# The last addition of a fused block is made by TensorE in PSUM instead of by VectorE

## The chip, the cores and the metric

The kernel runs on one core of one Trainium2 chip. A core has a matrix engine (TensorE, PE in the profile; its weight loads are PEld), three engines for element work (VectorE or DVE, ScalarE or ACT, GpSimd or POOL) and an engine that issues most DMAs (SyncE or SP). All have their own instruction lists and wait for one another by semaphores. The metric is the device time of one execution in microseconds; less is better.

## The reference, cut to what matters

`x` has 16 batches of 256 rows of 128 numbers. The block is an attention of the delta-rule kind with gates, and then a layer in which each row goes to one of eight experts:

```python
x = x + ga * attn(layernorm(x) * (1 + ca) + sa)
h = layernorm(x) * (1 + cb) + sb
route = softmax(h @ router_w + router_b)
y = (silu(h @ w1[e][:, :512]) * (h @ w1[e][:, 512:])) @ w2[e]     # e: the row's best expert
x = x + gb * (y * max(route))
```

`ga` and `gb` are gates, one vector of 128 numbers for each batch. The change concerns the last line, for half of the rows.

## The kernel before, in words

The 256 rows of a batch are cut into two slices of 128 rows, s = 0 and s = 1. A slice holds 16 tiles of 128 rows (one for each batch). The attention runs as a scan over time in which all engines take part; it fills the first two thirds of the span. Behind it comes the expert layer. The rows of a slice are sorted by expert into 23 padded tiles of 128 rows (NF = 23, so G = 46 tiles in all), with scatters to DRAM (`sorted_h`). For each tile g SyncE loads the rows, TensorE turns them (`turn_x`, L888), multiplies by the expert's first matrix (`hidden`, L900), ScalarE and VectorE make the gated product, TensorE multiplies by the second matrix (`second`, L917), VectorE copies the result out of PSUM (L2012), and GpSimd scatters the tile's rows back to their places in DRAM (`placed_y`, L1143).

When all tiles of a slice are back in DRAM, its 16 tiles are loaded again in four quarters q = 0 to 3 of four tiles, 256 KB each (`load_y`, L326), into YG. VectorE then finishes each quarter (`finish`): for slice 1 a product with the gates GB, which already hold the routing weight (L2027), and a sum with the residual rows XG (L2030). SyncE stores the quarter (`store_out`, L330). For slice 0 this happens while the tiles of slice 1 run. For slice 1 it is the end of the program: nothing else is left to do.

Each engine's list is written out by hand, and its order in the program is the order in which that engine works. The order between engines comes from semaphores alone: `y_in` (a quarter has landed), `dve_link` (VectorE's product is written and its own sum may read it), `out_ready` (a quarter is ready), `att_ps` and `x1_ready` (used earlier for the attention's results, four times for slice 1). At the end TensorE's list has nothing behind the last tile's `second`, and ScalarE's nothing behind the last `silu` (L1494).

Another line matters for prices: `project` (L636) multiplies 128x128 weights by 512 columns, three times for each of NB = 8 blocks; it is the form that the new matmuls have. `copy_x1` (L1360) is ScalarE's copy of one PSUM bank of 512 columns into four tiles of X, made for slice 0.

PSUM has eight banks of 128 x 512 numbers, bank[0] to bank[7]. The expert layer uses banks 0 and 4 for turned rows, 1, 2, 6 and 7 for the first product, 3 and 5 for results.

Of the kernel before, what the change touches and what calls it, by code (L numbers as in the profile page):

```python
# [8 lines left out]
ALU = mybir.AluOpType  # L9
ACT = mybir.ActivationFunctionType  # L10
# [8 lines left out]
def adaln_block(nc, x, Wq, Wk, Wv, Wo, Wbet, Wf, norm_w, router_w, router_b, w1, w2, c, wmod, out):  # L19
# [81 lines left out]
    with ExitStack() as ctx:  # L101
        def sb(name, shape, dt=F32):
            return ctx.enter_context(nc.sbuf_tensor(name, shape, dt))
# [3 lines left out]
        def sem(name, h=None):  # L107
            key = name if h is None else f"{name}{h}"
            if key not in sems:
                sems[key] = ctx.enter_context(nc.semaphore(key))  # L110
            return sems[key]
# [27 lines left out]
        ID = sb("ID", [P, P])  # L139
# [45 lines left out]
        bank = [ctx.enter_context(nc.psum_tensor(f"bank{i}", [P, 512], F32)) for i in range(8)]  # L185
# [4 lines left out]
        BACK_BANKS = [[bank[4]] * 4, TURN_BANKS[1]]  # L190
        LG_BANK = [bank[5][:, 0:NT * E], bank[0][:, P:P + NT * E]]
        RANK_BANK = [bank[4], bank[4]]


        def turned(g):
            return bank[4 if g >= TWO_X and g % 2 else 0][:, 0:P]
# [4 lines left out]
        def place_before(g, two):  # L201
            return g - 2 if g > two else g - 1
# [5 lines left out]
        def staged_k(h, n):  # L208
# [18 lines left out]
        YG = [[K_[h][:, s * P:(s + 1) * P, :].rearrange("p t d -> p (t d)").rearrange("p (n d) -> p n d", n=HB)  # L227
               for h in range(NHALF)] for s in range(NTIME)]
# [4 lines left out]
        XG = [X[:, :, :].rearrange("p (b s) d -> p s b d", s=NTIME)[:, s, :, :] for s in range(NTIME)]  # L233
# [18 lines left out]
        GB = WOG  # L252
# [73 lines left out]
            queue.dma_start(YG[s][q // 2][:, q % 2 * 4:q % 2 * 4 + 4, :], rows).then_inc(sem(f"y_in{q}"), 16)  # L326

        def store_out(queue, s, q):
            queue.wait_ge(sem("out_ready"), 4 * s + q + 1)
            queue.dma_start(out_t[s][:, 4 * q:4 * q + 4, :], XG[s][:, 4 * q:4 * q + 4, :]).then_inc(sem("stored"), 16)  # L330

        def shifted(queue, k):
# [140 lines left out]
        def _(sp):  # L473
# [116 lines left out]
            for q in range(4):  # L590
                store_out(sp, 1, q)
# [4 lines left out]
        def _(pe):  # L596
# [143 lines left out]
            def attend(s, q):  # L740

                h = q // 2
                if q % 2 == 0:
                    pe.wait_ge(sem(f"ot_in{h}_", s), 16 * (SHARE if (s, h) == (1, 0) else HB))
                if s == 1 and q == 0:
                    pe.wait_ge(sem("ot_pool0_", 1), 16 * (HB - SHARE))
                if s == 1 and q == 0:
                    pe.wait_ge(sem("pos_ready"), 1)
                    pe.wait_ge(sem("oh_ready"), 1)
                if s == 1 and q >= 2:  # L750
                    pe.wait_ge(sem("x1_ready", 1), q - 1)
                for i in range(4):
                    b = 4 * q + i
                    ps = ATT_BANKS[s][q][:, i * P:(i + 1) * P]
                    m = pe.matmul(ps, OT[h][:, b % HB, :], WOG[:, b, :], start=True, stop=(s == 1))
                    if s == 0:
                        m = pe.matmul(ps, ID[:, :], XG[0][:, b, :], start=False, stop=True)
                m.then_inc(sem("att_ps", s), 1)

            def turn_rows2(k):  # L760

                s, q = divmod(k, 4)
                if s == 0 and q >= 2:
                    pe.wait_ge(sem("router_in"), 4 * (q - 1))
                elif s == 0 or q < 2:
                    pe.wait_ge(sem("xn2_ready", s), 4 * (q + 1))
                if k == 0:
                    pe.wait_ge(sem("x1_ready", 0), 4)
                if s == 0 and q >= 2:
                    shifted(pe, k - 2)  # L770
                elif s == 1 and q >= 2:
                    pe.wait_ge(sem("act_rows"), NT // 2 + q - 1)
                for i in range(4):
                    m = pe.transpose(TURN_BANKS[s][q][:, i * P:(i + 1) * P], XNB[:, 4 * q + i, :], ID[:, :])
                m.then_inc(sem("xn2t_ps"), 1)
# [30 lines left out]
            def rank(s):  # L806
# [4 lines left out]
                else:  # L811
                    pe.wait_ge(sem("act_rows"), NT // 2 + 3)
                ohf = oh[:, :, :].rearrange("p t e -> p (t e)")
                pe.matmul(RANK_BANK[s][:, 0:NT * E], LOWER[:, :], ohf, start=True, stop=True)
                pe.matmul(RANK_BANK[s][:, NT * E:2 * NT * E].rearrange("p (e t) -> p e t", e=E), ONES[:, :],
                          oh[:, :, :].rearrange("p t e -> p e t"), start=True, stop=True).then_inc(sem("rank_ps"), 1)
# [65 lines left out]
            def turn_x(g):  # L882
                pe.wait_ge(sem(f"xs_in{g % XR}"), 16 * (g // XR + 1))
                if g == TWO_X:
                    pe.wait_ge(sem("pos_ready"), NTIME)
                elif g >= 1:
                    pe.wait_ge(sem("xst_ready"), place_before(g, TWO_X) + 1)
                pe.transpose(turned(g), XS[:, g % XR, 0:D], ID[:, :]).then_inc(sem("xt_ps"), 1)  # L888
# [17 lines left out]
            def second(g):  # L906
                s, j = divmod(g, NF)
                if j == 0:
                    pe.wait_ge(sem("tex_ready"), s + 1)
                expert = pe.value_load(tex[s][0:1, j:j + 1], min_val=0, max_val=E - 1)  # L910
                pe.wait_ge(sem("gu_ready"), g + 1)
                if g == TWO_Y:
                    pe.wait_ge(sem("act_rows"), NT // 2 + 4)
                elif g >= 1:
                    pe.wait_ge(sem("ys_ready"), place_before(g, TWO_Y) + 1)
                for c in range(FC):
                    m = pe.matmul(result(g), GU[g % 3][:, c * P:(c + 1) * P], W2[:, bass.ds(expert, 1), c, :],  # L917
                                  start=(c == 0), stop=(c == FC - 1))
                m.then_inc(sem("y_ps"), 1)

            for g in range(2):
                turn_x(g)
            for g in range(G + 2):
                if g == NF:
                    second(g - 2)
                    for k in range(2):
                        turn_x(g + k)
                if g < G:
                    hidden(g)
                if g == F_ATTEND[1] + 1:  # L930
                    for q in (2, 3):
                        attend(1, q)
                if g == F_TURN + 1:
                    for q in (0, 1):
                        turn_rows2(4 + q)
                if g == F_TURN + 2:
                    for q in (0, 1):
                        weigh_experts(4 + q)
                        turn_rows2(6 + q)
                if g == F_TURN + 3:  # L940
                    for q in (2, 3):
                        weigh_experts(4 + q)
                if g == F_ROUTE + 1:
                    rank(1)
                    turn_x(g + 2)
                if g >= 2 and g != NF:
                    second(g - 2)
                if g == F_ATTEND[0]:
                    for q in (0, 1):
                        attend(1, q)  # L950


        @block.gpsimd
# [204 lines left out]
        def _(act):  # L1158
# [367 lines left out]
            for g in range(G):  # L1526
# [17 lines left out]
                if g == NF - 1:  # L1544
                    exponentials(1)


        @block.vector
        def _(dve):
# [310 lines left out]
            def totals(s):  # L1860

                ranks, at = RANK_BANK[s], 3 * NT * E
                return ranks[:, NT * E:2 * NT * E], ranks[:, at:at + E]

            def sort(s):

                ranks = RANK_BANK[s]
                first = ranks[:, 2 * NT * E:2 * NT * E + E]
# [16 lines left out]
            def sorted_places(s):  # L1885

                ranks = RANK_BANK[s]
                first = ranks[:, 2 * NT * E:2 * NT * E + E]
# [125 lines left out]
            def finish(s, q):  # L2014

                if s == 0 and q == 0:
                    dve.wait_ge(sem("gb_in"), 16)
                dve.wait_ge(sem(f"y_in{q}"), 16 * (s + 1))
                yg = YG[s][q // 2]
                if s == 0:  # L2020
                    for b in range(4 * q, 4 * q + 4):
                        last = dve.scalar_tensor_tensor(out=yg[:, b % HB, :], in0=yg[:, b % HB, :], scalar=maxp[s][:, b:b + 1],
                                                        in1=GB[:, b, :], op0=ALU.mult, op1=ALU.mult)
                else:

                    y4 = yg[:, q % 2 * 4:q % 2 * 4 + 4, :]
                    last = dve.tensor_tensor(y4, y4, GB[:, 4 * q:4 * q + 4, :], ALU.mult)  # L2027
                link(last)
                xr = XG[s][:, 4 * q:4 * q + 4, :]
                dve.tensor_tensor(xr, xr, yg[:, q % 2 * 4:q % 2 * 4 + 4, :], ALU.add).then_inc(sem("out_ready"), 1)  # L2030
# [5 lines left out]
            for g in range(G + 3):  # L2036
# [14 lines left out]
                if g - 1 in F_ATTEND:  # L2051
                    q = 2 * F_ATTEND.index(g - 1)
# [4 lines left out]
                if g - 2 in F_ATTEND:  # L2057
                    q = 2 * F_ATTEND.index(g - 2) + 1
# [58 lines left out]
```

## Time and profile before

| what | us |
|---|---|
| runs shown | 468.97, 472.88, 473.53 (median 472.88) |
| the profiled execution | 471.62 |
| its span | 469.9 |
| last matmul of the last tile ends | 455.1 |
| first quarter of slice 1 has landed | 461.72 |
| last sum on VectorE ends | 467.14 |

The profile is one execution of its own; its span runs from the first to the last instruction, and the execution's time has 1.7 us more around it. In rows of the profile "L2030" is line 2030 of the program, `out<-in` are tiles by the program's names, and an idle time stands with what ended it.

### The profile page before, as it was taken

To read this page: it belongs to the slowest core of one execution; us is meant where nothing else is said; L and a number is where in the kernel's file an instruction comes from. 1 tells how busy PE (TensorE), PEld (TensorE's weight loads), DVE (VectorE), ACT (ScalarE), POOL (GpSimd) and SP (SyncE) were. 2 spreads that over 40 slices of the span, in tenths; PEclk is the share of its full clock that TensorE was granted. 3 is DMA by queue.
4 is the path that set the end of the run, shared out by engine and by line. 5 is a ranking of instruction groups with operands and counts; after the bars stand their busy time and mean duration, and the time that the engine had idled before them with its cause. 6 is when DMAs were issued, how large, how long until landed. Compare 5 with 4: busy or idle time off the path is not lost.

```text
span 469.9 us, 8624 instructions
## 1 busy us (share of the span) xinstructions
PE 371.7 (79%) x2495; PEld 321.4 (68%) x2495; DVE 377.1 (80%) x1143; ACT 281.8 (60%) x634; POOL 276.1 (59%) x339
## 2 busy tenths in 40 slices
PE   3867861947979996892968957879799999999970
PEld 2322320746766776892967857879699998999970
DVE  4868999999999999999998899785718444469634
ACT  3698876857357565577655545374855557556520
POOL 1037235999999949839496288512284546563340
PEclk9979886788879998997896786999989999999995
DMA  8185979990000004905000004127311114155006
GB/s 230 37 117 102 115 111 131 127 114 1 0 1 1 1 1 160 353 27 116 21 0 2 0 13 129 48 63 169 117 30 38 42 37 112 44 163 143 31 34 179
DMA packets 49502, 37.13 MB, mean 79 GB/s; under 512 B 11088, under 2 KB 45200, under 8 KB 49328
## 3 DMA queue, kind: packets, MB, share of 16 engines
q1 hardware_dynamic: 46064, 30.39, 32.9%
q0 software_dynamic: 3392, 6.18, 4.2%
q8 instruction: 21, 0.34, 0.3%
q14 instruction: 25, 0.20, 0.2%
HBM read 17.36 MB, written 10.29 MB: 59 GB/s over the span
## 4 chain that ended last, share of the span: by engine, by line
DVE 33%; PE 29%; POOL 16%; issue 10%; ACT 5%; DMA 5%; SPq 1%; ACTq 0%; POOLq 0%; DVEq 0%
PE bank L900 10%; DVE U L1794 5%; DVE S L1807 5%; PE bank L917 5%; DVE p L1788 4%; DVE p L1801 4%; PE bank L693 3%; PE bank L636 3%; POOL sorted_h L1085 3%; POOL big L1019 3%; DMA sorted_h<-X,pos 2%; DVE big L1724 2%; DVE X L1726 2%; POOL X L987 2%; POOL placed_y L1143 1%
## 5 line engine op out<-in xcount | busy, mean ns | idle before, releaser
L693 PE MATMUL bank<-prod_o,ID 128*128 128x128 f32 x512 | 75.2, 308 | 28.9 <-POOL prod_o L315 17.0
L900 PE MATMUL bank<-Q,p 128*128 128x128 f32 x736 | 95.0, 277 | 0.0
L693 PEld LDWEIGHTS bank<-prod_o,ID 128*128 128x128 f32 x512 | 70.3, 219 | 31.7 <-POOL prod_o L315 20.3
L900 PEld LDWEIGHTS bank<-Q,p 128*128 128x128 f32 x736 | 89.9, 194 | 0.2
L1312 ACT ACTIVATE p<-S,GAM 128x64 f32<-128x64 f32 x126 | 48.6, 412 | 65.6 <-DVE S L1807 64.8
L308 POOL TENSOR_TENSOR prod_o<-Q,ST 128x1024 f32<-128x1024 f32 x28 | 60.0, 2142 | 29.9 <-PE bank L697 29.7
L1143 POOL DMA_INDIRECT placed_y<-Q,place x46 | 44.3, 964 | 51.4 <-DVE place L2000 15.3
L1507 ACT ACTIVATE p<-big 128x1024 f32 x46 | 48.5, 1057 | 42.0 <-PE bank L900 39.4
L1807 DVE TENSOR_REDUCE S<-p 128x64 f32<-128x320 f32 x126 | 55.4, 470 | 0.0
L1794 DVE TENSOR_REDUCE U<-p 128x32 f32<-128x288 f32 x128 | 51.8, 436 | 0.0
L1788 DVE TENSOR_TENSOR p<-S,bank 128x256 f32<-128x256 f32 x128 | 48.3, 405 | 0.7 <-ACT bank L1307 0.7
L1801 DVE TENSOR_TENSOR p<-U,bank 128x256 f32<-128x256 f32 x126 | 47.1, 405 | 0.0
L1085 POOL DMA_INDIRECT sorted_h<-X,pos x32 | 30.9, 965 | 20.5 <-issue 7.8
L636 PE MATMUL bank<-ph,WP 128*128 128x512 f32 x48 | 30.0, 775 | 13.5 <-ACT ph L1197 13.5
L2005 DVE TENSOR_TENSOR S<-S,bank 128x512 f32<-128x512 f32 x31 | 21.2, 685 | 18.7 <-PE bank L900 14.2
L917 PE MATMUL bank<-big,S 128*128 x248 | 33.6, 281 | 2.8 <-ACT Q L1514 2.8
L697 PEld LDWEIGHTS bank<-prod_o,ID 128*128 128x128 f32 x256 | 35.2, 213 | 0.0
L697 PE MATMUL bank<-prod_o,ID 128*128 128x128 f32 (+3 forms) x256 | 34.8, 284 | 0.0
L315 POOL TENSOR_TENSOR prod_o<-PD,U 128x128 f32<-128x128 f32 (+1 forms) x112 | 33.8, 341 | 0.0
L1998 DVE COPY Q<-bank 128x128 f32<-128x128 f32 x46 | 13.2, 287 | 25.6 <-PE bank L888 25.4
L917 PEld LDWEIGHTS bank<-big,S 128*128 128x128 f32 x248 | 30.7, 196 | 3.3 <-issue 3.3
L636 PEld LDWEIGHTS bank<-ph,WP 128*128 128x128 f32 x48 | 10.7, 241 | 27.7 <-ACT ph L1197 15.5
(265 smaller groups left out, 755.0 us busy)
## 6 DMA issues: line engine op xcount, KB each, us to landing
big<-in_L_ffn_w_dram SPq DMA_DIRECT2D x1, 4096.0 KB, 14.2
big<-big SPq DMA_DIRECT2D x16, 192.0 KB, 5.0
Q<-sorted_h SPq DMA_DIRECT2D x46, 64.5 KB, 2.0
sorted_h<-ZERO SPq DMA_DIRECT2D x2, 1472.0 KB, 18.5
X<-in_L_attn_x_dram SPq DMA_DIRECT2D x8, 256.0 KB, 4.5
big<-big SPq DMA_DIRECT2D x16, 128.0 KB, 5.3
K<-placed_y SPq DMA_DIRECT2D x8, 256.0 KB, 4.3
out_dram<-X SPq DMA_DIRECT2D x8, 256.0 KB, 2.4
```

Source lines behind the costliest of these rows:

```text
L308: engine.tensor_tensor(slot[:, 0:HD, :, :, :], q, states.unsqueeze(3).broadcast_to(full), ALU.mult)
L636: m = pe.matmul(bank[1 + i][:, :], WP[:, i, :], rhs, start=True, stop=True)
L693: pe.matmul(ps, ID[:, :], prod_o[:, k % 2, i, :], start=(i == 0), stop=False, skip_group_check=True)
L697: m = pe.matmul(o4, ID[:, :], r4, start=False, stop=(d == C - 1), skip_group_check=True)
L900: m = pe.matmul(bank[(1, 6)[g % 2] + k][:, c * P:(c + 1) * P], W1E[g % 2][:, f:f + P], XST[:, g % 3, :], start=True, stop=True)
L917: m = pe.matmul(result(g), GU[g % 3][:, c * P:(c + 1) * P], W2[:, bass.ds(expert, 1), c, :], start=(c == 0), stop=(c == FC - 1))
L1143: pool.indirect_dma_start(placed_y[g // NF], bass.IndirectOffsetOnAxis(ap=place[:, g:g + 1], axis=0), YS[:, g % YR, :], None).then_inc(sem ...
L1312: act.activation(p2[h][:, :, :, C], S_[h][:, n % SR, :, :], ACT.Copy, scale=GAM[h][:, n:n + 1])\
L1788: dve.tensor_tensor(p1[h][:, n % UR, :, :, 0:HD], s_, w, ALU.mult).then_inc(sem("seq_w", h), 1)
L1794: dve.tensor_reduce(U_[h][:, n % VR, :, :], p1[h][:, n % UR, :, :, :], AX_X, ALU.add)\
L1801: dve.tensor_tensor(p2[h][:, :, :, 0:C], u, k, ALU.mult).then_inc(sem("state_in", h), 1)
L1807: dve.tensor_reduce(S_[h][:, (n + 1) % SR, :, :], p2[h][:, :, :, :], AX_X, ALU.add).then_inc(sem("s_ready", h), 1)
```

## The change

For slice 1 alone. TensorE gets eight more matmuls behind its last tile. Four (`residuals`) multiply the identity by the residual rows of a quarter, 512 columns, into banks 0, 4, 1 and 2, and open an accumulation there; they wait for nothing. Four (`add_results`) each wait until VectorE has multiplied the quarter by the gates, and multiply the identity by that product into the same bank, so that it is added to the residual rows. VectorE's sum of slice 1 is gone, and so is its wait for its own product; `out_ready` now comes from the product. ScalarE copies each finished bank into X behind its last `silu`, and the stores of slice 1 wait for these copies. Loads, stores and slice 0 stay as they are.

```diff
+        OUT_BANKS = [bank[i][:, :] for i in (0, 4, 1, 2)]
...
         def store_out(queue, s, q):
-            queue.wait_ge(sem("out_ready"), 4 * s + q + 1)
+            if s == 0:
+                queue.wait_ge(sem("out_ready"), q + 1)
+            else:
+                queue.wait_ge(sem("x1_ready", 1), 4 + q + 1)
...
+            def residuals(q):
+                pe.matmul(OUT_BANKS[q], ID[:, :], XG[1][:, 4 * q:4 * q + 4, :], start=True, stop=False)
+
+            def add_results(q):
+                pe.wait_ge(sem("out_ready"), 4 + q + 1)
+                pe.matmul(OUT_BANKS[q], ID[:, :], YG[1][q // 2][:, q % 2 * 4:q % 2 * 4 + 4, :], start=False, stop=True)\
+                    .then_inc(sem("att_ps", 1), 1)
...
+            for q in range(4):
+                residuals(q)
+            for q in range(4):
+                add_results(q)
...
+            for q in range(4):
+                act.wait_ge(sem("att_ps", 1), 4 + q + 1)
+                act.activation(XG[1][:, 4 * q:4 * q + 4, :], OUT_BANKS[q].rearrange("p (n d) -> p n d", n=4), ACT.Copy)\
+                    .then_inc(sem("x1_ready", 1), 1)
...
                     y4 = yg[:, q % 2 * 4:q % 2 * 4 + 4, :]
-                    last = dve.tensor_tensor(y4, y4, GB[:, 4 * q:4 * q + 4, :], ALU.mult)
+                    dve.tensor_tensor(y4, y4, GB[:, 4 * q:4 * q + 4, :], ALU.mult).then_inc(sem("out_ready"), 1)
+                    return
```

VectorE's list at the end of the program before, with what each instruction waits for (K is the tile that holds YG, X holds the residual rows):

```order
L2027 TENSOR_TENSOR K<-K,ph 128x512 [waits y_in0]
L2030 TENSOR_TENSOR X<-X,K 128x4x128 [waits dve_link]
L2027 TENSOR_TENSOR K<-K,ph 128x512 [waits y_in1]
L2030 TENSOR_TENSOR X<-X,K 128x4x128 [waits dve_link]
L2027 TENSOR_TENSOR K<-K,ph 128x512 [waits y_in2]
L2030 TENSOR_TENSOR X<-X,K 128x4x128 [waits dve_link]
L2027 TENSOR_TENSOR K<-K,ph 128x512 [waits y_in3]
L2030 TENSOR_TENSOR X<-X,K 128x4x128 [waits dve_link]
```

And the same place now (the program's lines have moved down by 22 there):

```order
L2049 TENSOR_TENSOR K<-K,ph 128x512 [waits y_in0]
L2049 TENSOR_TENSOR K<-K,ph 128x512 [waits y_in1]
L2049 TENSOR_TENSOR K<-K,ph 128x512 [waits y_in2]
L2049 TENSOR_TENSOR K<-K,ph 128x512 [waits y_in3]
```

The sums are gone and the products stand directly behind one another. TensorE's list at its end now, behind the last tile (L921 is `second`; before, the list ended with it):

```order
L921 ISA
L921 MATMUL bank<-big,S 128x128
L921 ISA
L921 MATMUL bank<-big,S 128x128
L928 MATMUL bank<-X,ID 128x512 x4
L932 MATMUL bank<-K,ID 128x512 [waits out_ready] x4
```

The four matmuls of L928 carry no wait and follow the tile at once; those of L932 wait for VectorE's products one by one.

## Rows read from the trace of the kernel before

**Rows 1.** The page: the span, and TensorE's granted clock in 40 slices.
```profile
span 469.9 us, 8624 instructions
...
PEclk9979886788879998997896786999989999999995
```

**Rows 2.** The chain of waits, 459 to 470 us: start, us, what.
```profile
461.74 0.70 DVE K L2027
...
462.47 0.69 DVE X L2030
...
463.80 0.69 DVE X L2030
...
465.12 0.69 DVE X L2030
...
466.45 0.69 DVE X L2030
```

**Rows 3.** Timeline of SyncE's queue, 466.9 to 469 us: start, us, line, operation.
```profile
467.17 0.37 SPq L330 DMA_DIRECT2D out_dram<-X  x1
```

**Rows 4.** Line L330, the stores: from issue to landing.
```profile
DMA to landing us min/median/max: 2.3/2.4/2.4
```

**Rows 5.** Line L326, the loads, 455 to 470 us: issue (ns, first and last start), landing.
```profile
L326 SPq DMA_DIRECT2D K<-placed_y x4: 370/504/507, 458.8 to 460.3; - x4
...
DMA to landing us min/median/max: 3.4/4.2/4.4
```

**Rows 6.** Timeline of TensorE, 455 to 470 us: all that it holds.
```profile
454.83 0.28 PE L917 MATMUL bank<-big,S 128*128 x1
```

**Rows 7.** Stretches of TensorE: length, busy time (instructions), granted clock, DMA share, GB/s.
```profile
26.20:30.50 4.30, 0.00 (x0) 0.91 1.12 137
30.60:36.50 5.90, 5.90 (x7) 0.50 0.67 70
...
45.40:46.70 1.30, 1.30 (x3) 1.00 1.14 132
46.80:50.10 3.30, 3.30 (x5) 0.50 1.15 131
65.90:67.90 2.00, 0.00 (x0) 1.00 0.35 40
...
281.40:285.70 4.30, 4.30 (x20) 0.50 0.32 100
337.50:340.20 2.70, 0.00 (x0) 1.00 0.10 24
340.40:343.70 3.30, 3.30 (x16) 0.50 0.06 20
...
459.90:469.80 9.90, 0.00 (x0) 0.50 0.73 210
```

**Rows 8.** Line L636, whole run, then 29 to 37 us: ns min/median/max.
```profile
L636 PE MATMUL bank<-ph,WP x48: 592/594/1219, 15.7 to 70.2; 128*128 128x512 f32 x48
...
L636 PE MATMUL bank<-ph,WP x6: 1057/1057/1219, 30.5 to 35.0; 128*128 128x512 f32 x6
```

**Rows 9.** Timeline: six passes of L636 at full clock, two weight loads at half.
```profile
53.05 2.74 PE L636 MATMUL bank<-ph,WP 128*128 128x512 f32 x6
...
31.55 0.33 PEld L636 LDWEIGHTS bank<-ph,WP 128*128 128x128 f32 x1 [0.52 <-issue]
32.40 0.33 PEld L636 LDWEIGHTS bank<-ph,WP 128*128 128x128 f32 x1 [0.52 <-issue]
```

**Rows 10.** The chain of waits, 308.5 to 309.8 us: VectorE to TensorE and back.
```profile
308.98 0.14 issue
309.11 0.32 PE bank L888
309.43 0.02 issue
```

**Rows 11.** Line L1360, ScalarE's copy of a bank to X.
```profile
L1360 ACT ACTIVATE X<-bank x4: 587/597/629, 225.4 to 232.0; 128x512 f32<-128x512 f32 x4
```

## The prediction

> **What bounds the kernel now.** The page comes first [rows 1]: the span is 469.9 us, no engine fills it, and no engine's share says what the last microseconds cost. They are read from the chain of waits [rows 2]. After TensorE and VectorE have finished the last tile, GpSimd's last scatter lands in DRAM; SyncE then issues four loads, and the first one's landing, at 461.72, starts VectorE. From there the chain is VectorE alone: a product, 0.02 us, a sum, and the next product overlapping the sum's end, four times, a period of 1.33 us (462.47, 463.80, 465.12, 466.45 are the sums' starts). The last sum ends at 466.45 + 0.69 = 467.14. SyncE issues the last store at 467.17 [rows 3] and it lands 2.3 us later [rows 4], at 469.47; 0.4 us of closing semaphores end the span. So what the change can move is the 5.42 us from 461.72 to 467.14, with 2.7 us of landing and closing behind it.
>
> Two other rows limit what can be won there. The loads are issued at 458.8 to 460.3 and land in 3.4 to 4.4 us [rows 5]: the fourth at about 460.3 + 4.4 = 464.7. So no chain can multiply the last quarter before 464.7; today VectorE reaches it at 465.73 (the last sum's start less 0.72), about 1 us after it came. And TensorE, which the change brings in, does its last pass from 454.83 to 455.11 [rows 6] and is idle from there to the end, at half clock from 459.9 on [rows 7].
>
> **What is removed.** Four sums on VectorE of 0.69 us each, and four waits of a sum for its product. VectorE's four products then start as fast as it takes them or as the loads land: the first is ready at 462.44, and the last at about 464.7 + 0.69 = 465.4, against the last sum's 467.14 now. That is the most there is to win, 1.75 us, and what comes behind the product has to fit in it.
>
> **What is added, first half: the residual rows.** Four matmuls of 128x512 with the identity, which wait for nothing and are queued directly behind TensorE's last tile. Their price is the projection's, L636, the only 128x512 form in the trace. Its source line stands at 24 matmuls in the program (three for each of eight blocks) and 48 records in the trace [rows 8]: an fp32 matmul runs in two passes. At full clock six passes take 2.74 us [rows 9] with a last one of 0.59, so (2.74 - 0.59) / 5 = 0.43 us per pass and 0.86 per matmul. Four matmuls are 8 passes, 3.4 us, from 455.1 to about 458.6. I cost them at nothing: VectorE's first product isn't there before 462.44, and nobody else waits on TensorE. Were all of it at half clock (6.8 us) it would end at 461.9 and still be covered.
>
> **What is added, second half: the results.** Four more such matmuls, each waiting for its product; these are on the path. Behind the first one stand the other three, ScalarE's copies wait for them in turn, and SyncE's stores for the copies. The hand-over from VectorE to a waiting TensorE was 0.14 us with its weight load, and back 0.02 [rows 10]. So the first starts at 462.44 + 0.14 = 462.58. What the eight passes take depends on the clock. At half clock the weight loads of the passes, which follow the passes one for one, start 0.85 us apart (31.55, 32.40) [rows 9], and a pass takes 1.06 when its end is counted in, the first of a stretch 1.22 [rows 8].
>
> The clock at 462.58 is the question. TensorE will have idled 4.0 us, from 458.6. In the trace there are 13 stretches of 2.4 us and more without a matmul between 26 us and 341 us, of which [rows 7] shows the first and the last; half clock came in each of them or at most 1.4 us after work resumed (45.4 to 46.7 was that longest delay, still at full clock). The idle stretch of 2.0 us at 65.9 left the clock alone. A stretch of 4.0 belongs to the first kind. Once down, the clock stayed there under full work for 3.3 us (340.4 to 343.7), 4.3 us (281.4 to 285.7) and 5.9 us (30.6 to 36.5) before it rose. So:
> - Longest: half clock through all eight passes. 462.58 + 0.16 (first pass) + 7 x 0.85 + 1.06 = 469.75.
> - Shortest: 1.4 us at full clock (3.3 passes), 3.3 us at half (3.9), the last 0.8 at full (0.35 us): 5.05 us, and 0.16 for the end of the last pass: 467.8.
> - Middle: half for 4.3 to 5 us (5.0 to 5.9 passes), the rest at full (1.3 to 0.9 us): about 5.8 us with 0.3 for the two ends: 468.7.
>
> In all three TensorE is later than the products (the last is ready at 465.4), so it, not VectorE or the loads, sets the end of this part. The Trainium skill, "TensorE: Matmul & The Clock Gate", section "Why this matters for your kernels", speaks against this placement: it counts idle gaps between bursts of matmuls as a way to lose the clock, and shows a loop whose matmuls all run cold behind a wait for a DMA. The trace agrees, by its thirteen stretches.
>
> **What is added, third: the copies out.** ScalarE's copy of one bank to rows of X is the form of L1360, 0.60 us [rows 11]; ScalarE is idle then. Three of the four lie beside TensorE's next matmul, the last is on the path. With 0.02 us before and after, the last store is issued 0.64 us after TensorE's end: at 470.4 (longest), 468.45 (shortest), 469.35 (middle), against 467.17 now. Its landing is costed as today, 2.3 us: the stores come 0.86 us or more apart, against 1.33 today, which showed no queueing; I allow the last 0.1 us behind the one before, inside the bounds. The sum: **+1.3 to +3.2 us, middle +2.3**. I take the middle, since nothing in the trace says where in a stretch the fall and the rise come.
>
> **The rivals.**
> - *TensorE keeps its full clock* (the other side: not slower). The residuals move its last work from 455.1 to 458.6, so the idle stretch shrinks from over 14 us to 4.0; if that is short enough, every pass takes 0.43. Then the loads bind: fourth product at 465.4, + 0.14, + 0.43 + 0.59 = 466.55, copy to 467.2, store at 467.2: +0.0 us. If the loads land half a microsecond sooner because no store runs beside them, -0.5. For it: the stretch of 2.0 us that left the clock alone. Against it: all thirteen longer ones, down to 2.4. It decides as soon as the clock is still full at about 464. Chance 0.12.
> - *TensorE doesn't load ahead of a wait.* If each result's first weight load stands behind its own wait and the hand-over isn't covered by the matmul in front, three more times 0.16 + 0.20 + 0.14 = 0.5 us come on top: up to 3.2 + 1.5 = +4.7 us, the 1% line. Against it: in [rows 9] the loads follow one another at the pace of the passes, without a gap of that size. Products 2 to 4 are ready before TensorE is free, so the waits are already met. Chance 0.05.
> - *A matmul of the identity takes one pass, not two.* Then the loads bind even at half clock: 465.4 + 0.14 + 1.22 (one first pass) + 0.64 gives 467.4, +0.2 us. Against it: 48 records for 24 matmuls in [rows 8]. Chance 0.02. The Trainium skill, "TensorE: Matmul & The Clock Gate", section "Back-to-back issue gap", gives one 512-column matmul 0.43 us at half clock, with which this case would be an estimated -0.2 us; the trace's 0.85 for each of two passes differs, and the measurement decides.
> - *Nothing moves*: each sum is taken out of VectorE's list and the stores wait for ScalarE, as the order shows, so that the change does less than it says I hold for nearly excluded; a fall of the clock that comes only after the last result falls under the first rival. Chance 0.01 for this and all that I don't see, at 0.
>
> **How the numbers follow.** The forecast, slower by 1.3 to 3.2 us, has 0.80. The profiled execution took 471.62 us, 1.7 above its span, and the sum gives 473.9 for it. The three runs shown have their median at 472.88, which makes 475.2; all four executions have theirs at 472.25, which makes 474.6, and that is my number. It is a change of 0.5%, and the runs of the same kernel lie 4.6 us apart (468.97 to 473.53), so about 1% is what a measurement here can tell from no change. The range takes the first rival from the profiled time's side (471.4) and the longest case on the slowest run less a little (476.4); outside it I leave 2 in 10. Slower by over 1% needs +4.7 us: the second rival, or the longest case with the runs' scatter: 0.09. Faster by over 1% has no mechanism, only scatter: 0.02. The rest, 0.89, is within 1%.
>
> **What would show it.** In the changed profile: four 128x512 matmuls (8 passes) right behind the last tile, ending near 458.6; VectorE's four products between 461.7 and 465.4; then eight passes on TensorE, most at half clock, that end near 468.7; the chain of waits ending in TensorE and one ScalarE copy, no longer in VectorE; the last store near 469.4. The prediction is wrong if the clock reads full between 462 and 466, if an fp32 128x512 matmul takes one pass, or if anything before 454 differs by more than the runs' scatter.

## The result, and the profile after

| | before | changed |
|---|---|---|
| median of 22 runs each, us | 471.78 | 473.43 |
| lowest to highest, us | 468.97 to 473.53 | 471.63 to 475.12 |
| span of the profiled execution, us | 469.9 | 472.2 |

The ratio is 1.0034, with a 95% interval of 1.0021 to 1.0048: slower by 1.6 us (1.0 to 2.3). A few executions took far longer, 516 to 932 us, and are left out everywhere; the longest was a profile of the changed kernel, in which a 128x128 matmul of `hidden` took 537 ns in the mean, against 278.

The chain of waits of the changed kernel, from 459 to 473 us (start, us, what), is to be read beside [rows 2]:

```profile
458.79 2.97 DMA K<-placed_y
461.76 0.02 issue
461.78 0.70 DVE K L2049
462.49 0.04 issue
462.53 6.23 PE bank L932 x8
468.76 0.02 issue
468.79 0.60 ACT X L1566
```

Up to 461.76 nothing differs from before: the first load is issued at 458.79 (before 458.76) and takes 2.97 us (before 2.96). Then the chain is no longer VectorE's eight pieces but one product, TensorE's eight passes, and one copy. TensorE's timeline (start, us, line, count, idle time before) has both halves of the addition:

```profile
454.97 3.60 PE L928 MATMUL bank<-X,ID 128*128 128x512 f32 x8
462.53 6.22 PE L932 MATMUL bank<-K,ID 128*128 128x512 f32 x8 [3.96 <-DVE K L2049]
```

The same eight passes take 3.60 us before the idle stretch and 6.22 us behind it. The stretches of TensorE (length, busy time, granted clock, DMA share, GB/s), to be read beside [rows 7], say why:

```profile
455.00:458.50 3.50, 3.50 (x10) 1.00 0.16 56
458.60:460.80 2.20, 0.00 (x0) 1.00 0.31 84
460.90:462.50 1.60, 0.00 (x0) 0.50 0.93 267
462.60:467.60 5.00, 5.00 (x6) 0.50 0.44 128
467.70:468.70 1.00, 1.00 (x3) 1.00 0.81 230
```

The granted clock fell from full to half 2.2 us into the idle stretch, before any result was there, and came back only for the last two passes. VectorE and SyncE in their timelines:

```profile
461.78 1.49 DVE L2049 TENSOR_TENSOR K<-K,ph 128x512 f32<-128x512 f32 x2 [6.32 <-DMA K<-placed_y]
464.22 1.45 DVE L2049 TENSOR_TENSOR K<-K,ph 128x512 f32<-128x512 f32 x2 [0.95 <-DMA K<-placed_y]
...
469.41 0.37 SPq L334 DMA_DIRECT2D out_dram<-X  x1
```

VectorE is done at 465.67 (464.22 + 1.45), 1.5 us earlier than before, and it now waits for landings (0.95 us before the third product). The last store is issued at 469.41, against 467.17 in [rows 3]: 2.24 us later, and the span is 2.3 us longer.

### The profile page after: what moved, and what is told of

It reads as the page before. It is cut to its first block, busy times and chain, and to the rows that moved or that the text cites. A ratio compares the mean times of both kernels' runs of the same rounds, so it can differ in the third digit from the quotient of the medians.

```text
span 472.2 us, 8656 instructions
## 1 busy us (share of the span) xinstructions
PE 378.6 (80%) x2511; PEld 322.8 (68%) x2511; DVE 375.2 (79%) x1139; ACT 283.4 (60%) x638; POOL 276.2 (58%) x339
## 4 chain that ended last, share of the span: by engine, by line
PE 31%; DVE 28%; POOL 14%; issue 11%; DMA 8%; ACT 6%; SPq 1%; ACTq 0%; POOLq 0%; DVEq 0%
PE bank L904 10%; DVE U L1816 6%; DVE S L1829 5%; DVE p L1810 5%; PE bank L921 5%; DVE p L1823 4%; PE bank L640 4%; PE bank L697 3%; POOL sorted_h L1102 3%; DMA XN<-ph 2%; POOL big L1036 2%; DMA sorted_h<-X,pos 2%; POOL prod_o L309 2%; PE bank L701 1%; POOL placed_y L1160 1%
## 5 line engine op out<-in xcount | busy, mean ns | idle before, releaser
L640 PE MATMUL bank<-ph,WP 128*128 128x512 f32 x48 | 31.5, 809 | 14.8 <-ACT ph L1214 14.7
L921 PE MATMUL bank<-big,S 128*128 x248 | 33.1, 278 | 2.7 <-ACT Q L1531 2.7
L640 PEld LDWEIGHTS bank<-ph,WP 128*128 128x128 f32 x48 | 11.7, 262 | 30.8 <-ACT ph L1214 16.8
L921 PEld LDWEIGHTS bank<-big,S 128*128 128x128 f32 x248 | 30.2, 193 | 3.3 <-issue 3.3
```

What stands on the lines that cost most here:

```text
L640: m = pe.matmul(bank[1 + i][:, :], WP[:, i, :], rhs, start=True, stop=True)
```

## The experiments

Times of a profile are given from the issue of the first of slice 1's last four loads, since executions reach that point up to 1 us apart. Ratios are to the kernel before, run beside. "Passes" are TensorE's passes for the results.

| kernel | ratio (95%) | idle before the first result | passes | last store issued |
|---|---|---|---|---|
| before, two profiles | 1 | | | 8.41 and 8.47 |
| changed, two profiles | 1.0034 (1.0021 to 1.0048) | 3.96, 3.97 | 8: 6.22, 5.46 | 10.62 and 9.88 |
| e1_warm | 1.0008 (0.9987 to 1.0029) | 0.57 | 8, in two groups: 1.99, 1.98 | 8.98 |
| e2_gap2 | 1.0028 (1.0002 to 1.0053) | 2.20 | 8: 5.40 | 9.77 |
| e5_results_only | 1.0060 (1.0037 to 1.0083) | 7.42 | 8: 5.88 | 10.30 |
| e6_half | 1.0013 (0.9996 to 1.0030) | 3.98 | 8, in two groups: 2.08, 2.08 | 8.99 |
| e3_split | 1.0040 (1.0018 to 1.0061) | | 4 | 9.16 |
| e7_order | 1.0023 (1.0005 to 1.0042) | | 4 | 8.61 |
| e4_pool | 1.0138 (1.0113 to 1.0163) | | none | 9.32 |
| e8_first | 0.9988 (0.9965 to 1.0011) | | 2 | 8.47 |

**e1_warm: the same change without the idle stretch.** The four residual matmuls are issued a second time, with the same output.

```diff
-            def residuals(q):
-                pe.matmul(OUT_BANKS[q], ID[:, :], XG[1][:, 4 * q:4 * q + 4, :], start=True, stop=False)
+            def residuals(q, alone=False):
+                pe.matmul(OUT_BANKS[q], ID[:, :], XG[1][:, 4 * q:4 * q + 4, :], start=True, stop=alone)
...
+            for q in range(4):
+                residuals(q, True)
             for q in range(4):
                 residuals(q)
```

> The four residual matmuls are issued twice, so that TensorE works from 455.0 to about 461.9 and idles 0.6 us instead of 4.0 before the first result. Theory (the half clock is the loss): the granted clock stays full, each result takes 0.86 us, the fourth quarter's landing at about 465.0 sets the end; the last store is issued at 467.2 to 467.5, 0.0 to +0.3 us against the kernel before (ratio 1.000 to 1.001) and some 2 us earlier than in the changed kernel's profile. Rival (the loss is the longer path of three engines and their hand-overs, whatever the clock): the last store stays near 469.4 and the ratio near 1.0034.

The chain of waits from the third load on, and two stretches of TensorE:

```profile
459.73 4.60 DMA K<-placed_y
464.33 0.02 issue
464.36 0.70 DVE K L2051
465.06 0.04 issue
465.10 2.00 PE bank L932 x4
467.10 0.02 issue
467.12 0.60 ACT X L1568
```

```profile
461.50:462.50 1.00, 0.47 (x2) 1.00 0.81 219
462.60:467.00 4.40, 3.83 (x8) 1.00 0.70 205
```

The clock stays full, four passes take 2.00 us, and the last store is issued at 8.98, 1.64 us and 0.90 us sooner than in the two profiles of the changed kernel, though TensorE does more work. That is the theory's case and not the rival's 10.6. It isn't the expected 8.4 to 8.7: the chain begins at the third load, which landed at 5.57 in this profile (5.17 and 5.48 in those of the kernel before), and the product, four passes and the copy follow it one after the other. The measured ratio's interval contains 1 and overlaps the changed kernel's a little, so the verdict against the changed kernel rests on the profile; e5_results_only below has a comparison by times.

**e2_gap2: an idle stretch of 2.2 us.** As e1_warm with two extra residual matmuls.

> Two of the four residual matmuls are issued twice, so that TensorE's idle stretch before the first result is about 2.2 us, between the one of 2.0 us that left the clock alone and the shortest of 2.4 us that took it. Theory: if the clock stays full, as e1 (0.0 to +0.3 us); if it falls, the eight passes are at half for 3.4 us and more and the last store comes at 468.5 to 469.4 (+1.3 to +2.3 us); nothing in between unless the fall comes after the first results. Rival (path length, not clock): near +1.6 us either way.

```profile
460.70:462.80 2.10, 0.00 (x0) 1.00 1.03 297
462.90:463.60 0.70, 0.70 (x2) 1.00 0.91 263
463.70:467.00 3.30, 3.30 (x5) 0.50 0.43 123
467.10:468.30 1.20, 1.16 (x3) 1.00 0.62 188
```

These stretches of TensorE show the late kind of fall: still full for the first 0.7 us of results, then half for 3.3 us, then full. The last store comes at 9.77, +1.3 us, the lower end of what was expected for a fall. So the clock also fell behind an idle stretch of 2.2 us. The time by itself doesn't separate this from the rival's +1.6 us; the clock in the rows does.

**e5_results_only: no residual matmuls.** The calls of `residuals` are taken out and the results start their banks themselves.

> The residual matmuls are left out, so the output lacks the residual rows of slice 1; all else is the changed kernel. Theory: the residuals are covered and their removal gives nothing; TensorE idles 7.4 us, the eight passes start at half clock as in the changed kernel and take 5.1 to 7.2 us: +1.3 to +3.2 us against before, ratio 1.003 to 1.007. Rival (the residual matmuls are on the path, or delay the results): the last store comes 0.5 us or more earlier than 469.4 although the clock is half.

```profile
461.70:466.00 4.30, 4.30 (x5) 0.50 0.45 131
466.10:467.50 1.40, 1.40 (x4) 1.00 0.42 124
```

With 7.42 us of idle time the passes begin at half clock and take 5.88 us; the last store comes at 10.30, between the changed kernel's two profiles. The residual matmuls are therefore covered: without them nothing is gained, and the measured ratio is, if anything, higher. This kernel was timed side by side with e1_warm: its interval begins at 1.0037, where that of e1_warm ends at 1.0029. Both have every product, hand-over, copy and store, and the one with fewer matmuls is the slower one. So the times, too, tell the results behind a long idle stretch from those behind a short one.

**e6_half: half the columns, every hand-over kept.** `OUT_BANKS[q][:, 0:2 * D]` and two of four tiles in `add_results`.

> The four result matmuls run over 256 of the 512 columns, so that half of slice 1's results is not added; every hand-over, copy and store stays. Theory (the passes at half clock are the price): a pass takes 0.43 us at half clock, TensorE keeps up with the products, the fourth landing at about 465.0 sets the end, the last store is issued near 467.6: +0.4 us against before (0.0 to +0.7), ratio 1.001, although the clock reads half. Rival (the path over three engines is the price): near +1.6 us as the changed kernel.

```profile
459.90:461.60 1.70, 0.00 (x0) 0.50 0.95 280
461.70:466.20 4.50, 4.08 (x8) 0.50 0.64 187
```

The clock is half throughout, and still the last store comes at 8.99, the same as in e1_warm with all columns at full clock. Halving the passes and doubling the clock do the same. What is left in both, some 0.5 us over before, is the path from the third load on: here too that load is the start of the chain (it landed at 5.48), and a product, four passes and a copy follow. How much of the 0.5 us is the path and how much a later landing isn't separated. As in e1_warm, the measured interval contains 1 and overlaps the changed kernel's.

**e3_split and e7_order: TensorE for two quarters only.** VectorE keeps its sums for quarters 2 and 3. In e7_order SyncE's last stores go out in the order 0, 2, 1, 3 as well:

```diff
-            for q in range(4):
+            for q in (0, 2, 1, 3):
                 store_out(sp, 1, q)
```

> TensorE and ScalarE do the first two quarters alone, VectorE keeps its sums for the last two. Theory: TensorE at half clock is done with the second quarter at about 466.3, its copy at 466.95; VectorE multiplies quarter 2 at 464.2 and ends the last sum at 467.0; last store near 467.0, -0.2 us against the kernel before (0.0 to -0.4), ratio 0.9995. Rival (the hand-overs cost as such): half of the loss stays, +0.8 us, ratio 1.0017.

> As e3_split, but SyncE's last four stores in the order of quarters 0, 2, 1, 3, so that the store of quarter 2 does not stand behind the wait for quarter 1. Theory (e3's loss was three stores in a burst behind that wait): quarter 2 is stored near 465.6, the last store near 467.3 and it lands 2.3 to 2.6 us later, 1.0 to 1.3 us sooner than in e3; against before +0.3 to +0.6 us, ratio 1.001. Rival (TensorE's work beside VectorE slows the sums or the stores): stays at e3's +1.9 us, ratio 1.004.

In e3_split VectorE's last sum ended at 8.06, 0.3 us sooner than before (0.1 had been worked out); but the last store was issued only at 9.16 and the kernel was slower by 1.9 us (0.8 to 2.9), which the theory misses and the rival's 0.8 just touches. SyncE takes its stores in order: that of quarter 2 stood ready behind quarter 1's, which TensorE and ScalarE released at 8.19, and then three went out in a row. Line L336 of e3_split (issue ns, first and last start, then landing), and of e7_order:

```profile
L336 SPq DMA_DIRECT2D out_dram<-X x4: 378/442/545, 465.2 to 467.9; - x4
...
DMA to landing us min/median/max: 2.3/2.6/3.2
```

```profile
L336 SPq DMA_DIRECT2D out_dram<-X x4: 372/443/545, 465.5 to 467.7; - x4
...
DMA to landing us min/median/max: 2.3/2.7/2.9
```

An issue took up to 0.55 us and a landing 3.2 us, against 0.37 and 2.3 where stores come apart. With the other order the last store was issued 0.55 us sooner and measured 1.1 us (0.2 to 2.0) over before. The expectation of 0.3 to 0.6 lies inside that, but so does the rival's 1.9, and the gain on e3_split, 0.8 us by the two ratios, is not clear of their intervals. So the burst's cost is shown by the profiles and not by the times: the last store lands at 12.3 in e3_split (9.16 + 3.2), 11.5 in e7_order (8.61 + 2.9) and 10.7 before (8.41 + 2.3). VectorE's sums took 0.69 us in both, as before, so they weren't slowed by TensorE's work.

**e4_pool: GpSimd instead of TensorE.** The kernel before, with GpSimd making the sums of quarters 0 and 2.

> The kernel before, with GpSimd in place of VectorE for the sums of quarters 0 and 2 of slice 1 (no matmuls, no copies). A GpSimd sum of this form took 1.2 us. Theory (only work that fits beside the landings helps): VectorE's last sum ends near 466.4 instead of 467.14, GpSimd's second near 466.2, the last store is issued near 466.6: -0.5 us against before (-0.2 to -0.8), ratio 0.999. Rival (sharing slows VectorE or GpSimd, or the landings bind): 0.0 us or slower, up to +0.5.

It was slower by 6.5 us (5.3 to 7.7), outside both expectations. Line L101 is the end of the program; its rows in e4_pool, and the one that differs in the kernel before (ns, start):

```profile
L101 POOLq DRAIN  x1: 10438/10438/10438, 466.3 to 466.3; - x1
...
L101 SPq COMPARE_BRANCH  x1: 42/42/42, 471.2 to 471.2; - x1
...
L101 SPq EVENT_SEMAPHORE  x1: 17/17/17, 476.9 to 476.9; - x1
```

```profile
L101 POOLq DRAIN  x1: 10668/10668/10668, 455.5 to 455.5; - x1
```

GpSimd's closing drain takes over 10 us. Before, it starts at 455.5 and is over at 466.1, beside VectorE's last work. With a sum that GpSimd starts only at 466.3 it runs to 476.7; SyncE had its last store landed at 471.2, and its list went on only at 476.9, 5.5 us of waiting later, when the drain was over. VectorE was slowed as well. Its timeline, and GpSimd's two sums:

```profile
463.17 1.74 DVE L2035 TENSOR_TENSOR K<-K,ph 128x512 f32<-128x512 f32 x1 [0.15 <-DMA K<-placed_y]
464.95 0.69 DVE L2041 TENSOR_TENSOR X<-X,K 128x512 f32<-128x512 f32 x1
...
466.88 1.64 DVE L2041 TENSOR_TENSOR X<-X,K 128x512 f32<-128x512 f32 x1
```

```profile
463.10 1.26 POOL L1162 TENSOR_TENSOR X<-X,K 128x512 f32<-128x512 f32 x1 [5.22 <-DVE K L2035]
466.32 1.65 POOL L1162 TENSOR_TENSOR X<-X,K 128x512 f32<-128x512 f32 x1 [1.96 <-DVE K L2035]
```

GpSimd's sums ran from 463.10 to 464.36 and from 466.32 to 467.97. The two of VectorE's instructions that were issued while one of them ran ended 0.55 us after it, at 464.91 and 468.52, and so took 1.74 and 1.64 us; the sum between them took 0.69. The Trainium skill, "SBUF — State Buffer", section "Who interferes with whom", has this as a shared pair of ports: a VectorE instruction with two inputs in SBUF is blocked by a GpSimd instruction that reads SBUF and was issued first. The trace agrees, by these two rows of VectorE.

**e8_first: TensorE for the first quarter only,** VectorE for the rest, stores in the order 1, 0, 2, 3.

> TensorE and ScalarE do the first quarter alone, VectorE keeps the other three sums; SyncE stores the quarters in the order 1, 0, 2, 3. Theory (a quarter taken off VectorE gains only as far as the last landing lets it, and TensorE at half clock has time for one quarter): VectorE's last sum ends 8.05 us after the first load's issue, against 8.38 in the kernel before; the last store is issued 8.1 us after it, against 8.41; -0.3 us against before (0.0 to -0.4), ratio 0.9994, which a measurement can't tell from 1. Rival (any use of TensorE at this place costs): +0.4 us or more, ratio over 1.001.

The ratio is 0.9988 (0.9965 to 1.0011), which can't be told from 1, as expected; but the profile doesn't have the 0.3 us either. The last store was issued at 8.47. VectorE waited 0.45 us for the third quarter, which landed at 5.67 in this profile, and went on from there without a pause to its last sum, which ended at 8.44. So the loads take what a freed VectorE gives. No version here is shown to beat the kernel before.

**The two kernels profiled again.**

> The kernel before, profiled a second time. The fourth load landed 5.94 us after the first load's issue in the first profile of it, and 6.03 to 6.32 in all the kernels profiled since. If the changed ends make the loads later, this one shows 5.9 again; if it is scatter of single profiles, 6.0 or more. The last store is issued 8.4 us after the first load's issue either way.

The fourth load landed at 6.24 in it, and the last store was issued at 8.47: the landing scatters by half a microsecond between single profiles (5.94 to 6.42 over all, and 5.17 to 5.67 for the third); this second profile of the kernel before lies inside both. That scatter is in each of the small differences above.

> The changed kernel, profiled once more. Theory (where the clock falls and rises moves from execution to execution): half clock at the first result or at most 1.4 us after it, eight passes in 5.0 to 7.2 us (6.22 in the first profile), the last store 9.9 to 11.6 us after the first load's issue (10.62 in the first). Rival (a fixed price per hand-over): again 6.2 and 10.6, within 0.1.

```profile
458.60:462.40 3.80, 0.00 (x0) 1.00 0.59 172
462.50:463.70 1.20, 1.20 (x3) 1.00 0.93 271
463.90:467.10 3.20, 3.20 (x5) 0.50 0.47 135
467.30:467.90 0.60, 0.60 (x2) 1.00 0.36 100
```

Here the clock outlasts the idle stretch, is full for the first 1.2 us of results, half for 3.2, then full again. The passes take 5.46 us and the last store is issued at 9.88. Two executions of one program differ by 0.76 us in these passes. Their idle stretches are the same to 0.01 us and VectorE's products to 0.15, so where the fall comes is what the rows show to be different.

## Why the prediction was right

The prediction, slower by 0.5% with 1.3 to 3.2 us, held: 0.34%, 1.6 us, and 473.43 us inside the range. Step by step:

- **What is to be won** was 1.75 us at most on VectorE; its last product ended at 465.67 where 465.4 was said, because the fourth load landed 0.25 us later. What comes behind the product took more than that, as forecast.
- **The residual rows cost nothing.** They ended at 458.57 (said 458.6). e5_results_only shows that taking them out gains nothing.
- **The price of a matmul** was right in its form: 16 records for eight matmuls, 0.43 us per pass before the idle stretch and 0.85 at half clock behind it. The rival of one pass is out: the rows show 1.71 us for the two passes of a matmul at half clock. The hand-over before the first result, put at 0.14 us, took 0.05. The Trainium skill, "TensorE: Matmul & The Clock Gate", section "Back-to-back issue gap", gives one 512-column matmul 0.43 us at half clock. For this fp32 matmul the trace differs, with 1.71, and the measurement decides.
- **The clock** fell and came back as argued from [rows 7]: in the first profile it fell in the idle stretch, in the second 1.2 us after work had resumed, where the prediction allowed up to 1.4. So its own sign of being wrong, a full clock between 462 and 466, was met for a part of that time in the second profile; the sign was put too narrowly for the shortest case in the same text. e1_warm, which removes only the idle stretch, takes 1.64 and 0.90 us off the last store of the two profiles; e6_half, which keeps the half clock and halves the columns, takes 1.63 and 0.89 off. Both leave every hand-over in place. So most of the loss is passes at half clock, and about 0.5 us of it stays in the path over three engines and the later landings.
- **The middle of the sum** was TensorE's end at 468.7 and the store at 469.35; the first profile shows 468.76 and 469.41. That it hit so closely is partly luck: the second profile has 0.76 us less, and the timed runs, +1.6, lie between the two (+1.4 in the last store of the second, +2.2 of the first). The term that was sized a little high is how long the clock stays down under the results: "half for 4.3 to 5 us" came out as 5.0 us in one execution and 3.2 in another, by the stretches above. The second is nearly the prediction's shortest case (1.4 us full, 3.3 half, the rest full; here 1.2, 3.2 and the rest). [rows 7] holds both kinds: where the clock had fallen in the idle stretch it stayed at half under work for 4.3 and 5.9 us (281.4 and 30.6), where it fell after work had resumed for 3.3 (46.8).
- **TensorE keeps its full clock**: out by both profiles. e1_warm shows what it would have given, near +0.5 us in the last store, not the 0.0 to -0.5 worked out: the loads landed later, not sooner, than reckoned (the fourth at 6.32, not 5.94), and the third's passes stood before the fourth's.
- **TensorE doesn't load ahead of a wait**: out. The weight loads of the changed kernel in their timeline:

```profile
463.55 0.34 PEld L932 LDWEIGHTS bank<-K,ID 128*128 128x128 f32 x1 [0.52 <-DVE K L2049]
464.40 0.34 PEld L932 LDWEIGHTS bank<-K,ID 128*128 128x128 f32 x1 [0.52 <-issue]
465.25 0.34 PEld L932 LDWEIGHTS bank<-K,ID 128*128 128x128 f32 x1 [0.52 <-DVE K L2049]
```

They are 0.85 us apart, the pass itself. The products of the second and third quarters were ready by then, at 463.27 and 464.91 in VectorE's timeline above, so these waits were met already, as the prediction argued, and nothing is added at a hand-over. In the second profile the third product was late for its turn: it was ready at 464.71, its load started at 464.76 beside the pass in front, and only about 0.1 us was added, not 0.5.

The absolute number was 1.2 us high. About 0.5 of that is the kernel before, whose median is 471.78 over 22 runs and not the 472.25 of the four executions used; the rest is the sum, 2.3 for 1.6.

## What to carry to other kernels

An engine brought in at the very end, behind a wait for a DMA, works at the price that it has after idling. For TensorE here a pass took twice as long while the clock was at half (0.85 us and not 0.43), and an fp32 matmul is two passes. Before giving a chain's work away, look at what would hold the chain up next. Here the fourth quarter landed only about 1 us before VectorE came to it, so a freed VectorE could start its last product at most 1 us sooner, and the path over three engines took its share of that. An order of stores that was free as long as one engine released them can become a queue when two do (e3_split). An engine whose closing work takes 10 us, as GpSimd's did here, is a poor choice for the last piece (e4_pool).

## What the runs showed of the hardware that was not expected

- GpSimd's closing drain lasted 10.4 to 10.7 us in every profile used here, covered in the kernel before and open in e4_pool.
- VectorE's 128x512 product or sum, issued while GpSimd made a sum of the same form, ended 0.55 us after GpSimd's and took 1.6 to 1.7 us; without, 0.69.
- Behind an idle stretch of 2.2 us TensorE's clock fell to half (e2_gap2), 0.7 us after work had resumed; behind one of 2.0 us, in [rows 7], it had not. That is one case of each.
- Three 256 KB stores issued in a row landed up to 3.2 us after their issue, and one issue took up to 0.55 us; apart they took 2.3 to 2.4 and 0.37.
